# A fused graph-attention and transformer kernel: attention output normalised by VectorE 32x32 transposes, products begun with the high half, a new order, and no products of ones

## The chip, the cores and the metric

The kernel runs on one core of a Trainium2 chip (trn2). The metric is device microseconds of that core for one execution; the median of the runs of the kernel before is 545.64 us. Engines: TensorE (PE) multiplies, its weight loads have rows of their own (PEld), VectorE (DVE), ScalarE (ACT) and GpSimd (POOL) do element-wise work, SyncE (SP) issues the DMAs. SBUF is the on-chip memory, PSUM holds what TensorE writes, in 8 banks of 128 x 512 words.

## What is computed

Eight batches `b` of a sequence of S = 256 rows by D = 256 features go through two layers, all in fp32:

```python
# layer 0: graph attention over the first 20 rows, H = 16 heads of 16
self_feat = [x, q] @ W_self.T + b_self
for d in range(2):                      # adjacency and its transpose
    aff = softmax(mask(qh . kh / 4) + label_bias)      # 256 x 16 x 20
    output += (aff @ kv) @ Wout[d] + bout[d]
x = x + relu(self_feat + output)
# layer 1: transformer block
nx = rmsnorm(x) * weight * (1 + scale) + shift
q, k, v = rope(nx @ wq + bq), rope(nx @ wk + bk), nx @ wv + bv
attn = softmax(q . k / 4) @ v           # 16 heads, 256 x 256 each
x = x + attn @ wo + bo
nx = rmsnorm(x) * weight2 * (1 + scale2) + shift2
x = x + (gelu(nx @ w_gate) * (nx @ w_up)) @ w_down      # D_FF = 1024
```

## The kernel before, in words

Each fp32 operand of a large product is split into a high half (rounded to fp32r) and a low half (the rest). `product` (L1485) makes a product of three fp32r matmuls per 128-deep slice of the contraction: high x high, high x low, low x high. ACT or DVE makes the high half, POOL mostly the low one (`xl`, `selfl`, `nxl`, `nzl`, `hlow`, all by `low`, L409), and TensorE waits for the low half before a product's first matmul.

The order of every engine's work is written out by hand as a list of steps: `head`, then `round_(it)` for it = 2 to 6, then `tail`, joined by `program`. A round works on four batches at once: layer 0 of batch it+1 (`selfm`, `kv0`, `q0`, `affm`) and the end of layer 0 of batch it (`pTt`, `y`, `x1T`), queries, keys and values of batch it (`qk`, `qkT`) and it-1 (`v`), attention of batch it-1 (`s`, `st`, `pv`) with the last heads of it-2, and the output product and feed-forward of batch it-2 (`wo`, `nzTr`, `gate`, `up`, `down`). Engines meet only by semaphores: each step waits for counters and adds to one.

Attention of one batch: `s(h)` (L1698) makes scores whose row maximum DVE takes (`mx`, L1178); `nmT` turns the negated maxima; `st(h)` (L1722) makes the transposed scores with the maximum folded in, ACT takes `exph` (L687), and `pv(g)` (L1737) multiplies four heads at a time with v, to which ones are appended so that the row sums come out too. The operands of `s` and `st` are two tiles, `kst` and `qst`, which SP rebuilds for each batch through DRAM (`store_hi`, `store_lo`, then the nine DMAs of `stack`, L288 and L291): `stack(b)` waits until `st(15)` of batch b-1 has read the tiles, and `s(0)` of batch b waits for all nine.

After `pv(3)` the output is still head by head and not divided by its sums. Before the change the way to `wo` is: ACT copies PSUM to `oT32` (`oc`, L693), TensorE transposes it in eight 128x128 blocks (`oT`, L1747), DVE takes reciprocals and multiplies (`onorm`, L1198, L1200) into `attn`, TensorE transposes back (`aT`, four blocks, L1542 by the helper `transposes`), ACT adds the bias and writes the high half (`ah`, L702), DVE the low half (`al`, L1207), and `wo` starts. Then `x2add` (L1217), `square2` (L713), `rms2` on POOL, `xr2_scaled` (L1129), `nzTr` (L1542), `nzc` (L722), `nzh`, `nzl`, and the feed-forward. `s(0)` of the next batch writes the PSUM bank that `oT` used, so it waits for `at_ok`.

`adjm` (L1024 to L1027) is DVE work of layer 0 that stands between `al` and `x2add` in each round. `warm(i, bank, n)` (L1531) issues n products of a 128x128 tile of ones with itself, whose result nobody reads: 15 such steps stand in the head, 7 in the tail, none in the rounds.

```python
def wo(c):
    def step(b):
        if b + 1 < B:
            pe.wait_ge(qk_ok.sem, qk_ok.at(b + 1, 1))
        else:
            pe.wait_ge(gelu_ok.sem, gelu_ok.at(b - 1))
        pe.wait_ge(al_ok.sem, al_ok.at(b))
```

## Time and profile before

| what | us |
|---|---|
| runs of the kernel before | 545.64, 543.8, 551.11 |
| the profiled execution, its own time | 545.3 |
| its span, first to last instruction | 543.5 |
| PE busy, share of the span | 487.7, 90% |
| DVE busy | 343.3, 63% |
| ACT busy | 250.3, 46% |
| POOL busy | 186.7, 34% |
| mean granted TensorE clock | 0.969 of full speed |

A matmul's row gives its latency, and matmuls overlap, so that busy time on PE is less than the sum of the rows. The steps of `program` give the stages: the head lasts to 123.7 us, the five rounds to 403.7 us (56.0 us each), the tail to the end. The first `pv(3)` of a batch is a good mark: in the middle rounds it comes at 294.98 and 351.03 us, one round apart.

### The profile page before, as it was taken

How to read it: one execution, taken by the hardware profiler on the slowest of the kernel's cores; microseconds unless marked ns; L12 is line 12 of the kernel's file. 1: busy time of each engine (PE TensorE's matmuls, PEld its weight loads, DVE VectorE, ACT ScalarE, POOL GpSimd, SP SyncE). 2: the span in 40 equal slices, each digit the busy share in tenths (PEclk: the TensorE clock that was granted, in tenths of full speed). 3: DMA queues.
4: the chain of work that ended last, by engine and by line, in shares of the span. 5: the costliest groups of instructions: out<-in, count | busy, mean ns of one | idle time of the engine just before them, and what ended most of it. 6: DMA issues, size and time to landing. Idle time of an engine off the chain costs nothing. (4 is left out here: it accounts for less than half of the span.)

```text
span 543.5 us, 10140 instructions
## 1 busy us (share of the span) xinstructions
PE 487.7 (90%) x3893; PEld 424.9 (78%) x3893; DVE 343.3 (63%) x612; ACT 250.3 (46%) x489; POOL 186.7 (34%) x170
## 2 busy tenths in 40 slices
PE   7978877888999899998999899989997998899887
PEld 7877776665899679967996799769976986697786
DVE  4865788685867686668766875787565843460211
ACT  2371341264437642763366336734663455327331
POOL 2074334154235323542354234422442240211022
PEclk9967998899999999999999999999999999889999
DMA  8460390009102720254024502370027006400000
GB/s 264 168 220 21 127 216 2 1 22 226 23 3 74 173 42 2 75 150 65 2 76 129 85 1 75 104 112 1 23 92 123 1 4 153 62 1 3 21 1 22
DMA packets 33424, 40.26 MB, mean 74 GB/s; under 512 B 3168, under 2 KB 28256, under 8 KB 33120
## 3 DMA queue, kind: packets, MB, share of 16 engines
...
q14 instruction: 16, 0.13, 0.1%
...
## 5 line engine op out<-in xcount | busy, mean ns | idle before, releaser
L1491 PE MATMUL ps<-splz,wh 128*128 128x256 f32 x512 | 99.2, 289 | 0.9 <-POOL splz L409 0.8
L1178 DVE TENSOR_REDUCE nm<-ps 128x2 f32<-128x512 f32 x128 | 84.4, 686 | 24.0 <-PE ps L1698 23.8
L687 ACT ACTIVATE ya<-ps 128x512 f32<-128x512 f32 x128 | 71.8, 597 | 31.6 <-PE ps L1722 29.8
L1491 PEld LDWEIGHTS ps<-splz,wh 128*128 128x128 f32 x512 | 81.2, 195 | 3.4 <-issue 3.3
L409 POOL TENSOR_TENSOR hs<-g,hs 128x512 fp32r<-128x512 f32 x32 | 41.3, 1292 | 98.4 <-ACT hs L745 98.4
L1491 PE MATMUL ps<-splz,wl 128*128 128x256 f32 x256 | 73.3, 286 | 0.0
L1698 PE MATMUL ps<-kst,qst 96*128 96x256 f32 x256 | 54.6, 313 | 6.3 <-DVE nm L1178 2.7
L1491 PE MATMUL ps<-wh,hs 128*128 128x256 f32 x256 | 54.3, 284 | 0.5 <-POOL hs L409 0.5
L1722 PE MATMUL ps<-qst,kst 100*128 100x256 f32 x256 | 49.5, 303 | 2.7 <-ACT ya L687 2.1
L1491 PEld LDWEIGHTS ps<-splz,wl 128*128 128x128 f32 x256 | 49.8, 195 | 0.0
L1698 PEld LDWEIGHTS ps<-kst,qst 96*128 96x128 f32 x256 | 40.0, 199 | 12.3 <-DVE nm L1178 6.7
L1722 PEld LDWEIGHTS ps<-qst,kst 100*128 100x128 f32 x256 | 37.0, 189 | 15.1 <-ACT ya L687 9.7
L1491 PEld LDWEIGHTS ps<-wh,hs 128*128 128x128 f32 x256 | 43.2, 191 | 1.0 <-POOL hs L409 0.6
L1491 PE MATMUL ps<-splx,wh 128*128 128x256 f32 x192 | 38.6, 296 | 3.2 <-DVE wl L992 2.1
L1229 DVE TENSOR_TENSOR g<-ps,g 128x512 f32<-128x512 f32 x32 | 21.9, 685 | 27.3 <-PE ps L1491 27.3
L1737 PE MATMUL ps<-ya,vv 128*32 128x256 f32 x512 | 34.3, 385 | 4.3 <-ACT ya L687 4.3
L1491 PE MATMUL ps<-wh,sply 128*128 128x256 f32 (+1 forms) x128 | 37.5, 352 | 0.3 <-issue 0.3
L1536 PE MATMUL ps<-onesr 128*128 128x128 f32 x261 | 36.4, 293 | 1.0 <-POOL onesr L391 1.0
L1536 PEld LDWEIGHTS ps<-onesr 128*128 128x128 f32 x261 | 34.6, 210 | 3.0 <-issue 2.0
L735 ACT ACTIVATE g<-ps 128x512 f32<-128x512 f32 x32 | 19.0, 594 | 37.7 <-PE ps L1491 37.7
L1491 PE MATMUL ps<-wl,hs 128*128 128x256 f32 x128 | 36.2, 283 | 0.0
L437 POOL TENSOR_TENSOR prob<-aff,arc 128x640 f32<-128x640 f32 x16 | 22.2, 1388 | 40.5 <-DVE arc L1097 24.9
...
## 6 DMA issues: line engine op xcount, KB each, us to landing
...
```

The costliest lines, as they stand in the source:

```text
L409: pool.tensor_tensor(into, whole, high.bitcast(FP32), ALU.subtract).then_inc(signal.sem, 1)
L437: pool.tensor_tensor(prob[:, :, 0:M], aff[:, c].rearrange("p d h m -> p (d h) m"), arc[:, c, :].unsqueeze(2).broadcast_to([P, 2 * H, M]), ...
L687: act.activation(ex[:, h % EXR], ps[:, h % 2].rearrange("p (c s) -> p c s", c=TC), ACT.Exp, scale=SCALE).then_inc(ex_ok.sem, 1)
L735: act.activation(g32[:, j % 2], ps[:, BANK["g"]].rearrange("p (k s) -> p k s", k=2), ACT.Gelu).then_inc(gelu_ok.sem, 1)
L1178: dve.tensor_reduce(nm[:, :, h], ps[:, h % 2].rearrange("p (c s) -> p c s", c=TC), AX.X, ALU.max, negate=True).then_inc(mx_ok.sem, 1)
L1229: dve.tensor_tensor(g, ps[:, BANK["u"]].rearrange("p (k s) -> p k s", k=2), g, ALU.mult).then_inc(hm_ok.sem, 1)
L1491: ins = pe.matmul(dst, lhs(a, k), rhs(c, k), start=first_ and n == 0 and m == 0, stop=last_ and n == len(ks) - 1 and m == 2, **kw)
L1536: pe.matmul(ps[:, bank, 0:P], onesr[:], onesr[:], start=True, stop=True)
L1698: ins = pe.matmul(ps[:, h % 2, c * S:(c + 1) * S], qst[0:96, h // 2, c * P:(c + 1) * P], kst[0:96, h, :], start=True, stop=True)
L1722: ins = pe.matmul(ps[:, h % 2, c * S:(c + 1) * S], kst[0:100, h, c * P:(c + 1) * P], qst[0:100, h // 2, :], start=True, stop=True)
L1737: ins = pe.matmul(ps[32 * j:32 * j + 32, BANK["o"], (g % 2) * S:(g % 2 + 1) * S], vv[b % 2][:, c, h, :], ex[:, h % EXR, c, :], start=c == ...
```

## The change

- **Normalisation.** `oc`, `oT` and `aT` are gone. DVE reads the PSUM of `pv` by one `dve.transpose` of 32x32 blocks (`ot(n)`, 128x512, twice a batch), takes reciprocals and multiplies in SBUF, and transposes back (128x256, twice a batch). `ah` and `al` are split in two halves and read SBUF. The rows of `wo` and of the bias are permuted on the host to fit.
- **High half first.** `product` issues the matmuls that need only the fresh operand's high half, then waits for the low half (`low()`), then the rest. Every product has one more wait, in its middle.
- **Last batch.** `rest(b)` gives batch 7 other buffers and banks for `wo` and the feed-forward. There, DVE makes the high and low halves of `hs` and the low half of `n` that ACT and POOL made.
- **Order.** All five lists are rewritten; `s(0)` of the next batch no longer waits for the normalisation, `nmT` waits for `o_ok`.
- **Products of ones.** All of `warm` is gone.

```diff
+        rest_before = Rest(splz, splz, nz32, x2, xr2, 5, 6)
+        rest_last = Rest(splx, sply, self32[:], x1, xr, 3, 4)
...
-            def oc(n):
...
-                    act.activation(oT32[:, 2 * n:2 * n + 2, :], ps[:, 2].rearrange("p (g s) -> p g s", g=2), ACT.Copy).then_inc(o_ok.sem, 1)
...
-            def ah(b):
-                act.wait_ge(aT_ps.sem, aT_ps.at(b))
...
+            def ah(n):
+                def step(b):
+                    act.wait_ge(aT_ok.sem, aT_ok.at(b, n + 1))
+                    if b == B - 1:
+                        act.wait_ge(q0_ps.sem, q0_ps.at(b))
...
+                    act.activation(rest(b).o[:, 0, n, :], aT[:, n], ident_fn, bias=vec[:, V_BV + n:V_BV + n + 1]).then_inc(ah_ok.sem, 1)
...
-            def onorm(c):
-                def step(b):
-                    dve.wait_ge(oT_ps.sem, oT_ps.at(b, c + 1))
...
+            def ot(n):
+                def step(b):
+                    dve.wait_ge(pv_ps.sem, pv_ps.at(b, 2 * n + 2))
+                    dve.transpose(ob[:, n].rearrange("p g b v -> p (g b v)"), ps[:, BANK["o"]]).then_inc(o_ok.sem, 1)
+                return step
+
+            def onorm(n):
+                def step(b):
+                    dve.wait_ge(o_ok.sem, o_ok.at(b, n + 1))
+                    dve.reciprocal(orc[:, n], ob[:, n, :, :, DH]).then_inc(orc_ok.sem, 1)
+                    dve.wait_ge(orc_ok.sem, orc_ok.at(b, n + 1))
+                    dve.tensor_tensor(attn[:].rearrange("p b g d -> p g b d"), ob[:, n, :, :, 0:DH],
+                                      orc[:, n].unsqueeze(3).broadcast_to([P, 2, S // 32, DH]), ALU.mult).then_inc(at_ok.sem, 1)
+                    dve.wait_ge(at_ok.sem, at_ok.at(b, n + 1))
+                    dve.transpose(aT[:, n], attn[:].rearrange("p b g d -> p (b g d)")).then_inc(aT_ok.sem, 1)
+                return step
...
             def hmul(j):
...
+                    if b == B - 1:
+                        dve.wait_ge(hm_ok.sem, hm_ok.at(b, j + 1))
...
+                        high(hs[:, j % 2, 0], g, hh_ok)
+                        dve.wait_ge(hh_ok.sem, hh_ok.at(b, j + 1))
+                        dve.tensor_tensor(hs[:, j % 2, 1], g, hs[:, j % 2, 0].bitcast(FP32), ALU.subtract).then_inc(hl_ok.sem, 1)
...
-            def product(dst, lhs, rhs, ks, first_=True, last_=True, **kw):
-
-                for n, k in enumerate(ks):
-                    for m, (a, c) in enumerate(((0, 0), (0, 1), (1, 0))):
...
+            def product(dst, lhs, rhs, ks, halves, low, first_=True, last_=True, **kw):
+
+
+                high_, low_ = halves
+                todo = [(k, at) for k in ks for at in high_] + [(k, low_) for k in ks]
+                for n, (k, (a, c)) in enumerate(todo):
+                    if n == 2 * len(ks):
+                        low()
+                    ins = pe.matmul(dst, lhs(a, k), rhs(c, k), start=first_ and n == 0, stop=last_ and n == len(todo) - 1, **kw)
                 return ins
+
+
+            FED, HELD = (((0, 0), (1, 0)), (0, 1)), (((0, 0), (0, 1)), (1, 0))
...
-            def warm(i, bank, n):
...
-                    pe.wait_ge(nxl_ok.sem, nxl_ok.at(b))
+                    pe.wait_ge(nxh_ok.sem, nxh_ok.at(b))
...
-                            range(KC)).then_inc(qk_ps.sem, 1)
+                            range(KC), HELD, lambda: pe.wait_ge(nxl_ok.sem, nxl_ok.at(b))).then_inc(qk_ps.sem, 1)
...
-                        pe.wait_ge(at_ok.sem, at_ok.at(b - 1, h + 1))
+                        pe.wait_ge(ex_ok.sem, ex_ok.at(b - 1, H - 1 + h))
...
-                    pe.wait_ge(al_ok.sem, al_ok.at(b - 1))
+                    pe.wait_ge(o_ok.sem, o_ok.at(b - 1))
...
-            def oT(c):
...
-            def aT(b):
...
-                        pe.wait_ge(gelu_ok.sem, gelu_ok.at(b - 1))
-                    pe.wait_ge(al_ok.sem, al_ok.at(b))
+                        pe.wait_ge(x1_ok.sem, x1_ok.at(b))
+                    pe.wait_ge(ah_ok.sem, ah_ok.at(b))
```

**PE around `pv(3)` of batch 3, in the middle rounds.** Before (L1737 is `pv`, L1621 `pTt`, L1747 `oT`, L1542 on `ya` `aT`, L1491 any `product`, on `sply` it is `v(1)`, on `splz` `wo`):

```order
L1737 MATMUL ps<-ya,vv 32x256 x8
L1621 MATMUL ps<-const_sb,prob 128x128 x4
L1747 MATMUL ps<-const_sb,ya 128x128 x8
L1621 MATMUL ps<-const_sb,prob 128x128 x4
L1542 MATMUL ps<-const_sb,ya 128x128 x4
L1491 MATMUL ps<-wh,sply 128x256
```

Now (L1779 is `pv`, L1663 `pTt`, L1538 `product`):

```order
L1663 MATMUL ps<-const_sb,prob 128x128 x4
L1779 MATMUL ps<-ya,vv 32x256 x8
L1663 MATMUL ps<-const_sb,prob 128x128 x4
L1538 MATMUL ps<-wh,sply 128x256
L1538 MATMUL ps<-wl,sply 128x256
```

Twelve transposes have gone, one `pTt` has moved ahead of `pv(3)`, and between `pv(3)` and the output product only one `pTt` and `v(1)` are left.

**PE a little later, up to `s(0)` of batch 4.** Before (L1632 is `y`, L1554 `rsum`, L1542 on `l` `x1T`, on `xr` `nzTr`, L1698 `s`; the products on `sply` are `v(0)`):

```order
L1632 MATMUL ps<-l,vblk 64x256 x8
L1554 MATMUL ps<-splx,onesr 128x256 x4
L1542 MATMUL ps<-const_sb,l 128x128 x4
L1491 MATMUL ps<-wh,sply 128x256
L1491 MATMUL ps<-wl,sply 128x256
L1491 MATMUL ps<-wh,sply 128x256 x2
L1491 MATMUL ps<-wl,sply 128x256
L1491 MATMUL ps<-wh,sply 128x256
L1698 MATMUL ps<-kst,qst 128x256 x2
L1542 MATMUL ps<-const_sb,xr 128x128 x4
```

Now (L1674 `y`, L1582 `transposes`, L1596 `rsum`, L1740 `s`):

```order
L1674 MATMUL ps<-l,vblk 64x256 x8
L1582 MATMUL ps<-const_sb,l 128x128 x4
L1596 MATMUL ps<-splx,onesr 128x256 x4
L1582 MATMUL ps<-const_sb,xr 128x128 x4
L1740 MATMUL ps<-kst,qst 128x256 x2
```

`v(0)` has moved from ahead of `s(0)` to behind it, and `nzTr` from behind it to ahead.

**DVE in the same place, from `asums(1)` to `x2add`.** Before (L1095 and L1097 are `asums`, L1103 `pTv`, L1198 and L1200 `onorm`, L1207 `al`, L1024 the first of `adjm`):

```order
L1095 TENSOR_REDUCE asum<-aff 128x32
L1097 RECIPROCAL arc<-asum 128x32
L1103 COPY l<-ps 128x4x128
L1198 RECIPROCAL orc<-ps 128x16
L1200 TENSOR_TENSOR ya<-ps,orc 128x256
L1198 RECIPROCAL orc<-ps 128x16
L1200 TENSOR_TENSOR ya<-ps,orc 128x256
L1103 COPY l<-ps 128x4x128
L1207 SCALAR_TENSOR_TENSOR splz<-ps,vec,splz 128x256 x2
L1024 TENSOR_TENSOR aff<-adjD,wb 128x880
```

Now (L1208 is `ot`, L1214, L1216 and L1219 `onorm`, L1110 `pTv`, L1225 `al`):

```order
L1110 COPY l<-ps 128x4x128
L1208 STREAM_TRANSPOSE ya<-ps 128x512
L1214 RECIPROCAL orc<-ya 128x16
L1216 TENSOR_TENSOR attn<-ya,orc 128x2x8x16
L1219 STREAM_TRANSPOSE ya<-attn 128x256
L1225 SCALAR_TENSOR_TENSOR splz<-ya,vec,splz 128x256
L1110 COPY l<-ps 128x4x128
L1225 SCALAR_TENSOR_TENSOR splz<-ya,vec,splz 128x256
L1031 TENSOR_TENSOR aff<-adjD,wb 128x880
```

`ot(0)` and `onorm(0)` stand earlier, on either side of `klow` and `result`; `ot(1)` and its `onorm` stand behind `asums(1)` and `pTv(0)`, and `adjm` is still ahead of `x2add`.

**PE at the end, batch 7.** Before, seven steps of ones stand around the chain:

```order
L1536 MATMUL ps<-onesr 128x128 x6
L1737 MATMUL ps<-ya,vv 32x256 x8
L1747 MATMUL ps<-const_sb,ya 128x128 x8
L1536 MATMUL ps<-onesr 128x128 x6
L1542 MATMUL ps<-const_sb,ya 128x128 x4
L1536 MATMUL ps<-onesr 128x128 x12
L1491 MATMUL ps<-wh,splz 128x256
```

Now `pv(3)` is followed by `wo` at once, which reads `splx`:

```order
L1764 MATMUL ps<-qst,kst 128x256 x4
L1779 MATMUL ps<-ya,vv 32x256 x8
L1538 MATMUL ps<-wh,splx 128x256
L1538 MATMUL ps<-wl,splx 128x256
L1538 MATMUL ps<-wh,splx 128x256
```

The two fillers behind `wo` (24 and 20 products) and the one ahead of the last two `down` (5) have gone as well.

## Rows read from the trace of the kernel before

**Rows 1.** The page, part 2: 40 slices of 13.6 us, granted clock in tenths.
```profile
PEclk9967998899999999999999999999999999889999
```

**Rows 2.** Windows: start:end, length, busy us (x instructions) by engine, PEclk, DMA.
```profile
291.74:347.79 56.05, 52.93 (x449) 46.19 (x448) 40.24 (x72) 29.42 (x59) 21.41 (x20) 1.00 0.29 71
...
294.99:307.89 12.90, 10.38 (x89) 7.97 (x89) 8.98 (x18) 3.99 (x10) 3.43 (x4) 1.00 0.84 163
307.89:351.03 43.14, 42.55 (x361) 38.22 (x359) 31.25 (x56) 25.44 (x49) 17.98 (x15) 1.00 0.13 43
```

**Rows 3.** Groups by shape: out<-in xcount | busy us, mean ns | idle before, releaser.
```profile
L1747 PE MATMUL ps<-const_sb,ya 128*128 128x128 f32 x64 | 8.5, 276 | 2.1 <-ACT ya L693 2.1
L1198 DVE RECIPROCAL orc<-ps 128x16 f32<-128x16 f32 x16 | 4.0, 251 | 18.9 <-PE ps L1747 18.9
L1200 DVE TENSOR_TENSOR ya<-ps,orc 128x256 f32<-128x256 f32 x16 | 6.8, 424 | 0.6
L702 ACT ACTIVATE splz<-ps,vec 128x256 fp32r<-128x256 f32 x16 | 6.7, 471 | 20.3 <-PE ps L1542 20.3
L1103 DVE COPY l<-ps 128x512 f32<-128x512 f32 x16 | 10.8, 672 | 6.2 <-PE ps L1621 6.0
L1536 PE MATMUL ps<-onesr 128*128 128x128 f32 x261 | 36.4, 293 | 1.0 <-POOL onesr L391 1.0
```

**Rows 4.** Timeline around the lull of batch 3: start, us, engine, line.
```profile
299.49 0.92 SPq L291 DMA_DIRECT2D kst<-qk_d  x2
301.34 1.06 DVE L1024 TENSOR_TENSOR aff<-adjD,wb 128x880 f32<-128x880 int32 x1
304.28 0.68 DVE L1217 TENSOR_TENSOR x<-ps,x1b 128x512 f32<-128x512 f32 x1
307.89 0.40 PE L1698 MATMUL ps<-kst,qst 96*128 96x256 f32 x2
308.23 0.63 PE L1542 MATMUL ps<-const_sb,xr 128*128 128x128 f32 x4
```

**Rows 5.** Timeline, the rebuilding of `kst` for batch 7.
```profile
459.88 0.93 SPq L291 DMA_DIRECT2D kst<-qk_d  x2
468.77 0.71 PE L1698 MATMUL ps<-kst,qst 96*128 96x256 f32 x4 [0.65 <-DMA kst<-qk_d]
```

**Rows 6.** Windows, columns as in rows 2: stretches around changes of the clock.
```profile
89.70:93.10 3.40, 1.27 (x11) 1.24 (x11) 3.26 (x7) 0.00 (x0) 0.00 (x0) 1.00 0.00 0
304.80:308.20 3.40, 2.33 (x20) 1.93 (x17) 2.20 (x7) 1.71 (x6) 2.16 (x3) 1.00 0.38 55
468.60:472.00 3.40, 2.73 (x14) 1.84 (x14) 3.25 (x7) 1.51 (x3) 0.38 (x2) 1.00 0.00 0
472.00:478.90 6.90, 6.55 (x29) 6.29 (x30) 2.84 (x5) 1.88 (x2) 1.00 (x1) 0.51 0.00 0
```

**Rows 7.** Timeline of the end, batch 7.
```profile
506.89 0.60 ACT L693 ACTIVATE ya<-ps 128x512 f32<-128x512 f32 x1 [1.19 <-PE ps L1737]
512.34 0.36 PE L1491 MATMUL ps<-wh,splz 128*128 128x256 f32 x1 [0.64 <-DVE splz L1207]
519.76 1.26 POOL L409 TENSOR_TENSOR splz<-g,splz 128x512 fp32r<-128x512 f32 x1 [3.02 <-DVE splz L955]
521.17 0.47 PE L1491 MATMUL ps<-splz,wh 128*128 128x256 f32 x2 [0.82 <-POOL splz L409]
537.08 0.67 PE L1536 MATMUL ps<-onesr 128*128 128x128 f32 x5
538.20 0.39 PE L1491 MATMUL ps<-wh,hs 128*128 128x256 f32 x1 [0.46 <-POOL hs L409]
```

**Rows 8.** Timeline of the head, queries and keys of batch 0.
```profile
56.75 1.27 POOL L409 TENSOR_TENSOR sply<-xr,sply 128x512 fp32r<-128x512 f32 x1 [2.96 <-DVE sply L955]
58.12 0.47 PE L1491 MATMUL ps<-wh,sply 128*128 128x512 f32 x1 [0.27 <-issue]
60.98 0.40 PE L1491 MATMUL ps<-splx,wh 128*128 128x256 f32 x2
```

More of the change, by code:

```diff
@@ L1 @@
+import collections
 import math
@@ L300, in store @@
                 sp.wait_ge(res_ok.sem, res_ok.at(b))
-                sp.dma_start(out[b].rearrange("(c p) d -> p c d", p=P), res[:]).then_inc(res_out.sem, 16)
+                sp.dma_start(out[b].rearrange("(c p) d -> p c d", p=P), rest(b).xr2[:]).then_inc(res_out.sem, 16)
             get_consts = fetch(consts[:], consts_in, consts_arr)
@@ L712, in square2 @@
                 for c in range(TC):
-                    act.activation(xr2[:, c], x2[:, c], ACT.Square, accum_out=ss2[:, c:c + 1]).then_inc(ss2_ok.sem, 1)
+                    act.activation(rest(b).xr2[:, c], rest(b).x2[:, c], ACT.Square, accum_out=ss2[:, c:c + 1]).then_inc(ss2_ok.sem, 1)
             def nzc(b):
@@ L1204, in al @@
-            def al(b):
-                dve.wait_ge(ah_ok.sem, ah_ok.at(b))
-                for k in range(KC):
-                    ins = dve.scalar_tensor_tensor(out=spla[:, 1, k, :], in0=ps[:, BANK["aT"], k * S:(k + 1) * S], scalar=vec[:, V_BV + k:V_BV + k + 1],
-                                                   in1=spla[:, 0, k, :].bitcast(FP32), op0=ALU.add, op1=ALU.subtract)
-                ins.then_inc(al_ok.sem, 1)
+                    dve.wait_ge(pv_ps.sem, pv_ps.at(b, 2 * n + 2))
+                    dve.transpose(ob[:, n].rearrange("p g b v -> p (g b v)"), ps[:, BANK["o"]]).then_inc(o_ok.sem, 1)
@@ L1211, in x2add, with al @@
+            def al(n):
+                def step(b):
+                    dve.wait_ge(ah_ok.sem, ah_ok.at(b, n + 1))
+                    dve.scalar_tensor_tensor(out=rest(b).o[:, 1, n, :], in0=aT[:, n], scalar=vec[:, V_BV + n:V_BV + n + 1],
+                                             in1=rest(b).o[:, 0, n, :].bitcast(FP32), op0=ALU.add, op1=ALU.subtract).then_inc(al_ok.sem, 1)
+                return step
             def x2add(b):
@@ L1216, in x2add @@
                     dve.wait_ge(w_low[part].sem, w_low[part].at(0, n + 1))
[L1217 removed]
+                dve.tensor_tensor(rest(b).x2[:], ps[:, rest(b).wo_bank].rearrange("p (c d) -> p c d", c=TC), x1b[:], ALU.add).then_inc(x2_ok.sem, 1)
             def nzh(b):
@@ L1221, in nzh @@
                 dve.wait_ge(wo_ps.sem, wo_ps.at(b))
-                high(splz[:, 0], nz32, nzh_ok)
+                if b == B - 1:
+                    dve.wait_ge(qk_ps.sem, qk_ps.at(b))
+                    dve.wait_ge(v_ps.sem, v_ps.at(b))
+                high(rest(b).n[:, 0], rest(b).n32, nzh_ok)
+                if b == B - 1:
+                    dve.wait_ge(nzh_ok.sem, nzh_ok.at(b))
+                    dve.tensor_tensor(rest(b).n[:, 1], rest(b).n32, rest(b).n[:, 0].bitcast(FP32), ALU.subtract).then_inc(nzl_ok.sem, 1)
             def hmul(j):
@@ L1528, in cond_2 @@
                 return step
-            def warm(i, bank, n):
-                def step():
-                    if i == 0:
-                        pe.wait_ge(onesr_ok.sem, onesr_ok.at(0))
-                    for _ in range(n):
-                        pe.matmul(ps[:, bank, 0:P], onesr[:], onesr[:], start=True, stop=True)
-                return step
             def transposes(dst, src, signal):
@@ L1983, in round_ @@
-                q0(1, 1)(it + 1)
-                up(3, 1)(it - 2)
-                q0(1, 0)(it + 1)
-                up(3, 0)(it - 2)
-                nxT(it)
-                affm(0)(it + 1)
-                st(0)(it - 1)
-                down(1, 0)(it - 2)
-                down(1, 1)(it - 2)
+                up(2, 0)(it - 2)
+                q0(0, 0)(it + 1)
+                s(15)(it - 1)
+                gate(3, 0)(it - 2)
+                gate(3, 1)(it - 2)
+                q0(1, 1)(it + 1)
@@ L1992, in round_ @@
+                q0(1, 0)(it + 1)
+                nmT(it - 1)
+                up(2, 1)(it - 2)
+                down(0, 0)(it - 2)
+                down(0, 1)(it - 2)
+                affm(0)(it + 1)
+                nxT(it)
+                up(3, 0)(it - 2)
+                down(1, 0)(it - 2)
+                st(0)(it - 1)
+                up(3, 1)(it - 2)
                 st(1)(it - 1)
@@ L2040, in tail @@
                 s(4)(6)
+                gate(0, 0)(5)
                 s(5)(6)
@@ L2043, in tail @@
                 s(6)(6)
-                gate(0, 0)(5)
                 s(7)(6)
@@ L2137, in tail @@
                 up(2, 0)(6)
+                gate(3, 1)(6)
+                nmT(7)
                 up(2, 1)(6)
-                nmT(7)
                 down(0, 0)(6)
+                down(0, 1)(6)
                 gate(3, 0)(6)
-                gate(3, 1)(6)
-                down(0, 1)(6)
                 up(3, 0)(6)
```

604 lines of the change are left out of this document (284 added, 320 removed).

## The prediction

> **What bounds the kernel now.** I read the page first, then windows by stage, then the timeline of one round, and last the timelines of the end and the head. The page's clock line shows TensorE at full speed from the fourth slice of the head on but for a few slices [rows 1]. A middle round takes 56.05 us, and PE is busy for 52.93 of them, DVE for 40.24, ACT for 29.42, POOL for 21.41 [rows 2]. So PE is the bound, but not evenly. From `s(0)` of batch 4 to the next `pv(3)` it is busy for 42.55 of 43.14 us: there only less PE work or a faster clock helps. From `pv(3)` of batch 3 to that `s(0)` it is busy for 10.38 of 12.90 us [rows 2]; I call this the lull. In it a chain sets the time: `pv(3)`, normalisation, `wo`, `adjm`, `x2add`, norm, `nzTr`. The reader is to see that all that the change takes from PE in a round, the twelve transposes, stands in the lull, where PE is not the limit, so that what counts there is when `s(0)` can come and not how much PE does.
>
> **Own time.** The profiled execution took 545.3 us, 1.8 more than its span of 543.5, and 0.3 less than the median of 545.64. The sum is made on 545.3.
>
> **The transposes in a round.** `oT` is eight transposes for each of eight batches, 8.5 us in all with 2.1 us of waiting [rows 3], so 1.3 us a batch; `aT` has half as many, 0.5 us at the same price. The way by DVE costs two transposes of 128x512 from PSUM, two reciprocals, two multiplications and two transposes of 128x256. The trace has no DVE transpose. The nearest row is the PSUM copy of 128x512 at 0.672 us [rows 3]; for 128x256 I take the multiplication's 0.424. From below I bound them by half of the copy, 0.34, from above by a GpSimd pass over 128x512, 1.27 us [rows 8]. I take the copy's price, being the same shape from the same bank.
> The page "Vector Engine (DVE) Microarchitecture Reference" of the Trainium skill, section 3.8, says that the 32x32 transpose passes one element per cycle and lane; no run here shows it yet, and by it the price would be about the copy's.
>
> The lull of one batch, counted from the start of `pv(3)`, which I take to come at the same point, since the exponentials ahead of it are the same: PSUM is complete after 1.2 us (at the end ACT, whose last exponential `pv(3)` needs, idles for 1.19 us until it can copy the result [rows 7]). `ot(1)` has `asums(1)` and `pTv(0)` ahead of it on DVE and starts at about 1.4; 0.67 for it, 0.25, 0.42 and 0.42 for the rest [rows 3] and some gaps bring 3.3; `ah(1)` at 0.47 [rows 3] brings 3.9, and the first `wo` starts. The low half (`al(1)`, behind `al(0)` and `pTv(1)`) is there at 4.8, after the four matmuls with the high half, a wait of 0.4. Behind `al(1)` DVE runs `adjm`, from 301.34 to 304.28 before [rows 4], 2.9 us, so `x2add` starts at 7.8. Before, it started at 304.28 - 294.99 = 9.3 [rows 2, 4]. From `x2add` to `nzTr` it was 308.23 - 304.28 = 3.95 us [rows 4] and stays that, since squares, `x1bias` and the norm are unchanged: `nzTr` at 11.75, and `s(0)`, now right behind, at 12.2 instead of 12.9. That is 0.7 us earlier. But `v(0)`, six matmuls at 0.12 (twelve of twice the columns take 60.98 - 58.12 = 2.86 us [rows 8]), 0.72 us, has moved from the lull into the dense part, and `nzTr`, four transposes, about 0.4, out of it. So the dense part grows by 0.3 and a batch gains about 0.4 us, not the 1.8 us of PE work removed. Six batches (0 to 5) have such a lull: -2.4 us.
> How much more could it be? `s(0)` needs `kst`, rebuilt after `st(15)`. At the end of the rounds it visibly waits for that: last pair issued at 459.88, `s(0)` at 468.77 with an idle time of 0.65 us put to the DMA, 8.9 us later [rows 5]. In the middle round the last pair goes out at 299.49 [rows 4]; 8.9 us more is 308.4, past the 307.89 at which `s(0)` started without such a wait, so this landing was quicker, but the room is small. `store` and `load_x_add`, which change places around `stack` in SP's list, are one DMA each and don't move it. I allow at most 1.0 us a batch, -6 in all, and at worst +1.1 a batch, +6.6, if the transposes take twice the copy.
>
> **The lull's clock.** This is the term against the change. The clock was at its upper level (2.4 GHz) in 89.70 to 93.10, with PE busy for 1.27 of 3.40 us, and at the lower one (1.2 GHz) right behind [rows 6]; it also fell after 468.60 to 472.00, where PE was busy for 2.73 of 3.40 us, for 6.9 us in which 29 matmul records took 6.55 us of PE. But it held through 304.80 to 308.20 at 2.33 of 3.40 [rows 6]. So the lulls were near the edge already, and now lose twelve transposes each. A fall costs half of the time spent at the lower level where PE is dense, 3.4 us of 6.9. I expect half of one such fall over the six lulls: +1.7 us. Bounds: 0, and six times 1.7 = +10.
> The page "TensorE: Matmul & The Clock Gate" of the Trainium skill says, in "What's actually happening", that the clock falls after an idle stretch. By that rule alone no lull would cost anything, since PE is never idle throughout one, and the sum would be 1.7 us less; the fall behind 468.60 to 472.00, at 2.73 busy of 3.40, speaks against it, and I keep the row's side.
>
> **High half first.** It adds one wait to each of 36 products a batch, in the middle of matmuls at 0.12 us. `s` and `gate` already have one or two waits each and, where those are satisfied, run at the same 0.12, so I take nothing; from above 0.02 us each would be 0.7 a batch and +5 in all. What it gives stands where a product waited for a low half: in the head `qk(0)` starts at 58.12, just after `nxl` (56.75 + 1.27) [rows 8], so up to -1.3. In the dense part PE waits for no low half, and it gives nothing.
>
> **Batch 6.** Its lull ends on the `kst` landing [rows 5], which no edit moves: 0. The filler behind `wo` goes; the clock fell there even with it.
>
> **The end.** After `pv(3)` of batch 7, PSUM complete at 506.89 [rows 7]: 0.67, 0.25, 0.42, 0.42, `ah` 0.47 and gaps of 0.2 put `wo` at 509.4, not 512.34: -2.9. `gate` no longer waits for POOL: it may start when that subtraction started, 519.76, instead of 521.17, -1.4, and then waits some 0.2 for DVE's low half, which is shorter. At the very end the last two `down` started 538.20 - 537.08 = 1.1 us after the ones ahead of them were issued [rows 7]; with the halves on DVE at about 0.45 and 0.7 they are in time: -1.1. Together -5.2. Against it: between `pv(3)` and the first `gate` PE now has twelve matmuls and four transposes in 10 us, less than the stretch that kept the clock up [rows 6]. So `wo` and the first gates run at the lower level. By the 6.9 us of the fall [rows 6] that is 3.4 us; with some of `wo`, +3.5. Bounds: 0 to +8.5, if it stays low for the whole feed-forward of 17 us. The end gives -1.7.
>
> **The head.** Fillers go from gaps, so their 36.4 us [rows 3] are no gain: they stood where PE waited. What they did was to hold the clock, which was at the upper level from 48.8 to 82.9. `qk(0)` and `qk(1)` of batch 0, from 58.12 to 60.98 [rows 8], stand on the chain to `s(0)`; at the lower level they take 2.9 us more. The four `q0` ahead of the first softmax (0.72 each) would add 2.9 too; since PE is dense there and the clock would recover on the way, half: 1.5. Less the 1.3 of the high half: +3.1. Bounds -3 (the clock holds, and the new DMA order helps) to +10 (everything PE does to 103 us is slower). Where DVE's row maxima pace the first `s`, the clock costs nothing.
>
> Sum: -2.4 + 1.7 + 0 - 1.7 + 3.1 = +0.7, 546.0 us.
>
> **The rivals.** First, *the chain pays more than I think*: DVE transposes are cheap, the lulls shrink by the full 1.0 us (-6), the clock holds in lulls and head (head -3), and the end keeps its -5.2. That is -14.2, 531.1 us. For it: idle time on DVE in the round (16 of 56 us), and an end in which all is chain. Against: the `kst` landing and the fillers, which stood where the clock was seen to fall. Chance 0.17.
> Second, *the clock decides, and the kernel is slower*. Place: the lulls, where the transposes no longer fill. Price: 1.7 us for a fall with one half of 3.4 us dense behind it. From the point at which the lulls fall in four of six batches (+6.8, and less the 1.7 counted) and the head pays the +8 of its clock, it is 546.0 + 5.1 + 4.9 = 556.0, and with all six and the end's 8.5 some 564. Chance 0.15 for more than 2% slower.
> Third, *the change to DVE does not relieve the bound at all*: the DVE chain behind `pv(3)` is late by `asums` and `pTv`, `s(0)` comes as before, and the round grows by `v(0)`: +0.3 a batch instead of -0.4, 550 us. It lies within my own case's range.
>
> **How the numbers follow.** My case, within 2% (534.7 to 556.6; about what a measurement of this kernel can tell from no change), 0.68; the first rival 0.17 beyond that on the fast side; the second 0.15 on the slow side. The forecast is 546 us. My case's bounds alone are 538 to 555. For 8 in 10 the range goes half way into both rivals: 533 to 560.
>
> **What would show it.** Right: rounds of 55 to 56 us; `s(0)` about 12.2 us behind `pv(3)`; DVE transposes of 128x512 near 0.67 us; the clock lower than 0.969 in the mean, with falls in the head and behind `pv(3)` of batch 7; the last `gate` stage starting 3 to 4 us nearer to `pv(3)`. Wrong: rounds under 54.5 us, which would mean that the dense part has shrunk, and I have nothing that shrinks it; or lulls at the lower clock in most rounds; or a row for a DVE transpose over 1 us; or products with a gap in the middle in the dense part.

## The result and the profile after

The changed kernel takes 548.76 us (median of 20 runs, 544.53 to 552.56), the kernel before beside it 545.26 us (20 runs, 542.88 to 552.18): a ratio of 1.006, 95% interval 1.0039 to 1.0081. It is slightly slower. The forecast was 546.0, "within 2%". The profiled execution took 548.7 us, with a span of 546.9.

The page of after, first the engines, then the clock line, the counterpart of [rows 1]:

```profile
PE 460.4 (84%) x3536; PEld 399.8 (73%) x3536; DVE 381.2 (70%) x653; ACT 240.3 (44%) x469; POOL 185.6 (34%) x165
...
PEclk9955957589999989999999989998999999999869
```

PE does 27 us less, DVE 38 us more. The clock line has more low digits in the head and near the end, and single 8s in the rounds, where the line of before had none.

Windows of after: the lull of batch 1 and the dense part behind it, which ran at full clock, the same pair of batch 3, whose dense part began at the lower clock, then four stretches at the lower clock: the one behind the lull of batch 4, two in the head, one at the end (start:end, length, busy us by engine, PEclk, DMA; a PEclk of 1.00 is 2.4 GHz, 0.50 is 1.2 GHz). They answer to [rows 2] and [rows 6].

```profile
189.04:201.66 12.62, 9.21 (x71) 7.25 (x71) 10.85 (x19) 2.84 (x8) 4.69 (x5) 0.86 0.69 138
201.66:245.74 44.08, 43.28 (x368) 38.95 (x367) 34.78 (x59) 25.71 (x49) 17.67 (x14) 1.00 0.16 52
303.98:316.95 12.97, 8.56 (x71) 6.52 (x71) 10.92 (x19) 2.85 (x8) 4.68 (x5) 0.97 0.78 126
316.95:362.19 45.24, 44.45 (x367) 40.11 (x365) 34.59 (x58) 25.71 (x49) 17.67 (x14) 0.97 0.16 51
...
374.20:377.60 3.40, 3.18 (x15) 3.21 (x16) 2.06 (x5) 1.22 (x3) 0.50 (x1) 0.50 0.00 0
29.50:56.80 27.30, 19.91 (x91) 17.15 (x90) 16.52 (x27) 11.09 (x22) 14.93 (x12) 0.50 0.37 127
70.40:87.50 17.10, 10.18 (x43) 9.51 (x44) 11.79 (x17) 5.25 (x10) 11.61 (x9) 0.50 0.88 158
514.20:527.80 13.60, 7.25 (x31) 6.65 (x32) 3.72 (x8) 4.05 (x9) 0.88 (x2) 0.50 0.00 0
```

The reader is to see three things. The lull is 12.6 to 13.0 us, against 12.90 before, although PE's work in it went from 10.38 to about 9: PE's work does not set its length, a chain does. The dense part grew from 43.14 to 44.08 us, and to 45.24 where its start ran at the lower clock (granted clock 0.97 in the mean; the fifth line shows such a stretch by itself, 3.40 us at 0.50, behind the lull of batch 4). And head and end have long stretches at 0.50.

The groups of after that took the place of `oT`, `aT` and the old `onorm` of [rows 3]:

```profile
L1216 DVE TENSOR_TENSOR attn<-ya,orc 128x256 f32<-128x256 f32 x16 | 13.4, 840 | 0.5
L1208 DVE STREAM_TRANSPOSE ya<-ps 128x512 f32<-128x512 f32 x16 | 11.4, 710 | 16.7 <-PE ps L1779 16.7
L1219 DVE STREAM_TRANSPOSE ya<-attn 128x256 f32<-128x256 f32 x16 | 7.1, 445 | 0.5
```

The transposes cost what was forecast (0.71 and 0.45 us for 0.67 and 0.42). The multiplication costs 0.84 us where the same shape cost 0.424 before. The timelines of POOL and of DVE in the lull of batch 3, the counterpart of [rows 4], show why:

```profile
305.99 1.30 POOL L418 TENSOR_TENSOR splx<-xT,splx 128x512 fp32r<-128x512 f32 x1
```
```profile
305.88 0.25 DVE L1214 RECIPROCAL orc<-ya 128x16 f32<-128x16 f32 x1
306.16 1.40 DVE L1216 TENSOR_TENSOR attn<-ya,orc 128x256 f32<-128x256 f32 x1
307.60 0.45 DVE L1219 STREAM_TRANSPOSE ya<-attn 128x256 f32<-128x256 f32 x1
```

The multiplication starts at 306.16, while GpSimd's `xl` runs until 307.29, and ends 0.27 us behind it. It is 1.40 us in batches 0 to 4; in batches 5 to 7, which have no `xl` beside it, it is 0.42. The first multiplication of a batch meets GpSimd too, for less long. In batch 3 (POOL, then DVE):

```profile
299.94 1.72 POOL L432 TENSOR_TENSOR aff<-aff,amx 128x640 f32<-128x640 f32 x1
```
```profile
301.33 0.62 DVE L1216 TENSOR_TENSOR attn<-ya,orc 128x256 f32<-128x256 f32 x1
```

It too ends 0.3 us behind the GpSimd operation. The multiplication of before, with one operand in PSUM, ran its first 0.24 us beside a GpSimd operation as well, and took no longer than its mean of 0.424:

```profile
296.79 1.27 POOL L437 TENSOR_TENSOR prob<-aff,arc 128x640 f32<-128x640 f32 x1 [3.13 <-PE ps L1621]
```
```profile
297.82 0.42 DVE L1200 TENSOR_TENSOR ya<-ps,orc 128x256 f32<-128x256 f32 x1
```

The end, for [rows 7] (PE, then DVE's first transpose behind `pv(3)`):

```profile
511.60 1.07 PE L1779 MATMUL ps<-ya,vv 128*32 128x256 f32 x16 [0.94 <-ACT ya L696]
515.37 0.55 PE L1538 MATMUL ps<-wh,splx 128*128 128x256 f32 x1 [2.70 <-ACT splx L707]
...
521.78 1.09 PE L1582 MATMUL ps<-const_sb,xr 128*128 128x128 f32 x4 [3.52 <-DVE xr L1141]
524.54 0.55 PE L1538 MATMUL ps<-sply,wh 128*128 128x256 f32 x1 [1.66 <-DVE sply L962]
```
```profile
512.74 0.72 DVE L1208 STREAM_TRANSPOSE ya<-ps 128x512 f32<-128x512 f32 x1 [2.65 <-PE ps L1779]
```

`wo` starts 3.77 us behind `pv(3)`, before 6.59; `gate` 12.94 us behind it, before 15.42.

For every trace I read the same marks off PE's timeline, the starts of `pv(3)`, `s(0)` and the last `down(3,1)` (us; "end" is `pv(3)` of b7 to the last `down(3,1)`, "lull" is `pv(3)` to `s(0)`, "dense" is `s(0)` to `pv(3)`):

| kernel | median | pv(3) of b0 | b0 to b5 | b5 to b7 | end | lull b3 | dense b2 |
|---|---|---|---|---|---|---|---|
| before | 545.26 | 126.78 | 280.27 | 98.70 | 33.27 | 12.91 | 43.15 |
| after | 548.76 | 132.34 | 288.00 | 91.25 | 30.83 | 12.97 | 44.08 |
| fill_lulls | 543.69 | 130.74 | 283.57 | 92.09 | 30.98 | 12.63 | 44.09 |
| fill_ends | 539.64 | 126.69 | 286.48 | 91.36 | 28.31 | 12.97 | 44.04 |
| before_bare | 550.88 | 130.45 | 280.64 | 99.07 | 36.31 | 12.90 | 43.17 |
| xl_early | 540.95 | 132.75 | 278.61 | 92.35 | 31.39 | 11.65 | 44.08 |
| dense_back | 546.69 | 130.50 | 285.66 | 92.68 | 30.94 | 12.98 | 44.01 |
| low_old | 557.85 | 133.22 | 293.23 | 94.28 | 32.31 | 14.74 | 44.88 |
| last_plain | 550.86 | 131.37 | 287.39 | 91.60 | 31.73 | 12.62 | 44.09 |
| combo1 | 537.44 | 127.18 | 281.81 | 92.13 | 28.42 | 12.38 | 43.97 |
| best2 | 535.51 | 130.02 | 278.64 | 92.91 | 28.39 | 11.64 | 44.09 |
| best3 | 540.66 | 127.23 | 285.86 | 92.25 | 28.33 | 12.25 | 45.11 |
| best4 | 539.37 | 128.39 | 281.76 | 92.86 | 28.41 | 12.17 | 44.52 |
| best5 | 528.72 | 128.37 | 275.08 | 93.24 | 28.43 | 10.66 | 44.10 |

From before to after the four stretches change by +5.56, +7.74, -7.45 and -2.44, in sum +3.4 us. The question for the experiments is what these four are.

### The profile page after: what moved, and what is told of

It is laid out like the page before. It is cut to its first block and busy times, and to the rows that moved or that the text cites. A ratio compares the mean times of both kernels' runs of the same rounds, so it can differ in the third digit from the quotient of the medians.

```text
span 546.9 us, 9419 instructions
## 1 busy us (share of the span) xinstructions
PE 460.4 (84%) x3536; PEld 399.8 (73%) x3536; DVE 381.2 (70%) x653; ACT 240.3 (44%) x469; POOL 185.6 (34%) x165
## 5 line engine op out<-in xcount | busy, mean ns | idle before, releaser
L1538 PE MATMUL ps<-splz,wh 128*128 128x256 f32 x448 | 97.4, 286 | 0.0
L1538 PEld LDWEIGHTS ps<-splz,wh 128*128 128x128 f32 x448 | 76.0, 190 | 0.3 <-ACT g L744 0.2
L1740 PE MATMUL ps<-kst,qst 96*128 96x256 f32 x256 | 56.9, 324 | 5.3 <-DMA kst<-qk_d 2.5
L1538 PE MATMUL ps<-splz,wl 128*128 128x256 f32 x224 | 58.3, 282 | 0.0
L1764 PE MATMUL ps<-qst,kst 100*128 100x256 f32 x256 | 52.7, 307 | 3.0 <-issue 1.7
L1538 PE MATMUL ps<-wh,hs 128*128 128x256 f32 x256 | 54.5, 283 | 0.0
L1740 PEld LDWEIGHTS ps<-kst,qst 96*128 96x128 f32 x256 | 42.3, 210 | 13.8 <-DVE nm L1189 7.4
L1538 PE MATMUL ps<-splx,wh 128*128 128x256 f32 x192 | 47.9, 321 | 5.1 <-DVE wl L999 3.9
L1538 PEld LDWEIGHTS ps<-wh,hs 128*128 128x128 f32 x256 | 43.3, 190 | 0.2
L1538 PEld LDWEIGHTS ps<-splx,wh 128*128 128x128 f32 x192 | 38.7, 228 | 6.4 <-issue 6.3
L1538 PEld LDWEIGHTS ps<-splz,wl 128*128 128x128 f32 x224 | 42.7, 191 | 0.0
L1538 PE MATMUL ps<-wh,sply 128*128 128x256 f32 (+1 forms) x128 | 41.0, 370 | 0.8 <-ACT xr L664 0.6
L1779 PE MATMUL ps<-ya,vv 128*32 128x256 f32 x512 | 34.3, 385 | 6.0 <-ACT ya L696 6.0
L1663 PE MATMUL ps<-const_sb,prob 128*128 128x128 f32 x128 | 22.8, 316 | 14.9 <-POOL prob L446 14.9
L1538 PE MATMUL ps<-wl,hs 128*128 128x256 f32 x128 | 33.4, 282 | 0.0
L432 POOL TENSOR_TENSOR aff<-aff,amx 128x640 f32<-128x640 f32 x16 | 23.5, 1467 | 23.1 <-DVE amx L1096 23.1
```

The source lines that it names most:

```text
L432: pool.tensor_tensor(t, t, amx[:, c, :].unsqueeze(2).broadcast_to([P, 2 * H, M]), ALU.subtract).then_inc(asub_ok.sem, 1)
L1538: ins = pe.matmul(dst, lhs(a, k), rhs(c, k), start=first_ and n == 0, stop=last_ and n == len(todo) - 1, **kw)
L1663: ins = pe.transpose(ps[:, BANK["pT"][d], g * P:(g + 1) * P], prob[:, at:at + 4, :].rearrange("p h m -> p (h m)"), ident)
L1740: ins = pe.matmul(ps[:, h % 2, c * S:(c + 1) * S], qst[0:96, h // 2, c * P:(c + 1) * P], kst[0:96, h, :], start=True, stop=True)
L1764: ins = pe.matmul(ps[:, h % 2, c * S:(c + 1) * S], kst[0:100, h, c * P:(c + 1) * P], qst[0:100, h // 2, :], start=True, stop=True)
L1779: ins = pe.matmul(ps[32 * j:32 * j + 32, BANK["o"], (g % 2) * S:(g % 2 + 1) * S], vv[b % 2][:, c, h, :], ex[:, h % EXR, c, :], start=c == ...
```

## The experiments

Fillers are products of ones, written as the old `warm`; all edits are to the changed kernel unless said otherwise.

**fill_lulls.**

```diff
                 pv(3)(it - 2)
+                warm(31, 0, 8)()
...
                 v(1)(it - 1)
+                warm(32, 0, 8)()
...
                 y(it)
+                warm(33, 0, 8)()
...
                 rsum(it + 1)
+                warm(34, 0, 8)()
```

> The changed kernel with products of ones put back, but only in the rounds, at four gaps of each lull (eight each: behind pv(3), v(1), y and rsum), 160 in all. Theory A, the clock costs the rounds 1.2 to 1.4 us for each of the four falls that follow a lull: the falls at 193, 258, 316 and 374 us go, s(0) to the next pv(3) takes 44.1 us in all rounds instead of 45.2 to 45.4, and the time is about 5 us below the changed kernel's 548.8, near 544. Theory B, the dense part has grown by moved work alone and the falls are harmless: the falls go and the time stays at 548 to 549. Theory C, the fillers run into the chain behind pv(3): the lulls grow by 0.3 us or more, and the time is 550 or more.

543.69 us, 0.9949 of before (0.9919 to 0.9979). Windows, to be held against the lull and the dense part at 303.98 and 316.95 of after:

```profile
300.85:313.48 12.63, 11.95 (x101) 9.89 (x102) 10.85 (x19) 2.88 (x8) 4.70 (x5) 1.00 0.72 130
313.48:357.56 44.08, 43.31 (x368) 38.99 (x366) 34.73 (x59) 25.71 (x49) 17.69 (x14) 1.00 0.15 52
```

Theory A. PE does 11.95 us in a lull that is no longer for it, and the clock holds through all rounds. Batch 0 to 5 takes 4.43 us less, three falls of 1.5 us. There were four in after; the one at 193.30 lies wholly in its lull, where PE waits anyway, and cost nothing (12.62 us, against 12.63 here).

**fill_ends.** Fillers in the head and the tail alone, at the gaps of the new order, for instance:

```diff
                 pv(3)(7)
+                warm(17, 0, 22)()
                 wo(0)(7)
                 wo(1)(7)
+                warm(19, 0, 26)()
```

> The changed kernel with products of ones put back in the head (about where they stood before, 175 of them) and in the last two lulls and the end (113), none in the rounds. Theory A, the clock: pv(3) of batch 0 comes at 127 to 128 us again instead of 132.3, the end gains 1.5 to 2 us, and the time is near 548.8 - 4.5 - 1.7 = 542.6. Theory B, the head is late by its new order of DMAs and steps and not by its clock: pv(3) of batch 0 stays at 131 to 132, and the time is 547 or more.

539.64 us, 0.9887 (0.9843 to 0.9931). Theory A, and more than expected: `pv(3)` of batch 0 is back at 126.69, so all of the head's 5.56 us went with the fillers; the end takes 28.31 us instead of 30.83. Two falls are left in the rounds, so that batch 0 to 5 takes 1.5 us less. The stretch from `pv(3)` to `gate`, which had a granted clock of 0.60 in after, now reads:

```profile
504.53:515.73 11.20, 10.28 (x95) 9.36 (x95) 4.55 (x11) 2.78 (x8) 0.88 (x2) 1.00 0.01 1
```

**before_bare.** The kernel before without any `warm`, for instance:

```diff
                 nzTr(7)
-                warm(20, 4, 20)()
                 gate(0, 0)(7)
```

> The kernel before with all its products of ones taken out and nothing else. Theory A: the head loses 4.5 us and the end 2 us, 545.3 + 6.5 = 552. Theory B, the fillers were worth nothing: 545.3. If this is as slow as 552, then what the changed kernel gains elsewhere is about 3 us.

550.88 us, 1.0093 (1.0059 to 1.0126), +4.6 us beside its own runs of before. The trace has +3.67 in the head and +3.04 in the end. Theory A, with the head less dear than in the changed kernel.

**xl_early.**

```diff
                 asub(1)(it)
+                xl(it + 1)
                 aprob(1)(it)
-                xl(it + 1)
                 x1bias(it - 1)
```

> The changed kernel with one line of GpSimd's list moved: the low half of x (xl of the next batch) goes out ahead of aprob(1) and not behind it, so that it no longer runs at the same time as VectorE's second multiplication of the normalisation. Theory A, the multiplication waits for the GpSimd subtraction that runs beside it: it takes 0.42 us again in batches 0 to 4 instead of 1.40, wo comes 1 us sooner, each lull ends up to 1 us sooner, and the time is up to 5 us lower, 544 to 546 (less where s(0) then meets the landing of kst). Theory B, the multiplication is slow by its own access pattern: it stays at 1.40 us and the time at 548 to 549.

540.95 us, 0.9901 (0.9863 to 0.9940): 7.8 us off after's 548.8 for one moved line. The group of the multiplication, and POOL and DVE in the lull of batch 3:

```profile
L1216 DVE TENSOR_TENSOR attn<-ya,orc 128x256 f32<-128x256 f32 x16 | 8.6, 535 | 0.5
```
```profile
297.60 1.47 POOL L418 TENSOR_TENSOR splx<-xT,splx 128x512 fp32r<-128x512 f32 x1
```
```profile
302.13 0.43 DVE L1216 TENSOR_TENSOR attn<-ya,orc 128x256 f32<-128x256 f32 x1
```

Theory A: 0.43 us with nothing beside it, and each lull exactly 0.97 us shorter (11.65). Against fill_lulls, which has no falls either, batch 0 to 5 takes 4.96 us less, five times 0.99. The rest of the gain is that no fall came in the rounds any more; I had not expected that, and why the clock held was not tested. PE does 8.19 us in such a lull of 11.65, and did 8.56 in one of 12.97.

**dense_back.**

```diff
-                pTt(1)(it)
                 pv(3)(it - 2)
+                pTt(1)(it)
...
                 rsum(it + 1)
+                v(0)(it - 1)
                 nzTr(it - 2)
...
-                v(0)(it - 1)
                 s(1)(it - 1)
```

The tail has the same two moves, for batch 5.

> The changed kernel with two of TensorE's steps put back from the dense part of a round into the lull, where they stood before: pTt(1) behind pv(3), and v(0) between rsum and nzTr (also in batch 5's lull). Theory A, the dense part grew by exactly these, 0.54 + 0.72 us, less the 0.38 of nzTr: s(0) to the next pv(3) falls from 44.1 to 42.8 us, the lull stays at 12.6, and as TensorE is busier in the lulls the falls behind them go too: 6 x 1.26 + 3 x 1.5 = 12 us, 537. Theory B, the lull is full already (v(0) ends late and holds s(0)): the lull grows by 0.7 us and the time is 544 to 549.

546.69 us, 1.0009 (0.9974 to 1.0045). Neither: the dense part stays, the falls in the rounds go, and the lull grows by half of what theory B says. The windows, and PE's waits in the dense part and at the `pv(3)` that ends it:

```profile
187.53:200.50 12.97, 9.47 (x80) 7.29 (x81) 11.21 (x19) 3.01 (x8) 4.86 (x5) 1.00 0.70 130
200.50:244.51 44.01, 42.45 (x359) 37.94 (x357) 34.70 (x59) 25.70 (x48) 17.68 (x14) 1.00 0.17 53
```
```profile
PE ps L1779 <- ACT ya L696: 1.1, 1, 1.1
PE ps L1538 <- POOL splz L418: 0.3, 1, 0.3
```

After has only the first of the two waits, and so had before:

```profile
PE ps L1779 <- ACT ya L696: 0.7, 1, 0.7
```
```profile
PE ps L1737 <- ACT ya L687: 0.5, 1, 0.5
```

PE does 0.83 us less in the dense part and the dense part stays at 44.0. In after, `pTt(1)` filled a part of the wait of `pv(3)` for the last exponential, and `v(0)` the wait of `gate(0,0)` for its low half. Take them out and the waits are 0.7 us longer. So the dense part was not bound by PE alone, though its busy share was 98%. The last `st` starts 42.5 us behind `s(0)` in after and 42.4 in dense_back, against 41.8 before: the way to the last exponential is longer by the same amount with the two steps and without them, and what in the new order lengthens it no run shows. In the lull `v(0)` then held up `nzTr` by 0.35 us.

**low_old.**

```diff
-                todo = [(k, at) for k in ks for at in high_] + [(k, low_) for k in ks]
+                todo = [(k, at) for k in ks for at in (*high_, low_)]
                 for n, (k, (a, c)) in enumerate(todo):
-                    if n == 2 * len(ks):
+                    if n == 0:
                         low()
```

> The changed kernel with product undone: the wait for the low half stands ahead of a product's first matmul again, and the matmuls go slice by slice; 36 waits in the middle of products are gone. Theory A (the prediction's): the waits cost nothing where they are satisfied, what high half first gives is 1.3 us at qk(0) of the head and 0.4 us in each lull and at the end: 548.8 + 1.3 + 2.8 = 553. Theory B: each wait in the middle costs 0.02 us, 5 us in all, and the time is 545 to 547 after what is lost in the lulls. Theory C: nothing either way, 548 to 549.

557.85 us, 1.0221 (1.0175 to 1.0267), 9.1 us over after, more than any theory had. PE's longest wait in the lull of batch 1 (in after it is the 1.2 us for the high half, ACT L707), and the two windows:

```profile
PE ps L1538 <- DVE splz L1225: 2.0, 1, 2.0
```
```profile
191.91:205.45 13.54, 9.31 (x71) 7.39 (x71) 10.94 (x19) 2.79 (x8) 4.69 (x5) 0.87 0.66 121
205.45:250.32 44.87, 43.75 (x371) 39.07 (x371) 34.84 (x59) 25.79 (x49) 17.68 (x14) 1.00 0.15 52
```

High half first is worth 0.9 us in this lull and 0.8 in this dense part. What the waits in the middle of products cost can't be read from this run, since it takes their gain away with them; the gain is larger in every stretch. The 9.1 us are not the waits for low halves alone. From `pv(3)` of batch 0 to that of batch 5 the clock is at the lower level for 23.9 us, in after for 13.7, so a part is the clock's. And in the dense part PE's wait for a low half is only 0.2 us, while PE is busy 0.5 us longer; the edit also changes the order of a product's matmuls, and no run parts the two.

**last_plain.** The last batch with the common buffers, banks and engines (`rest` gives `rest_before` for every batch), its steps on POOL and ACT in the order of before.

```diff
-            return rest_last if b == B - 1 else rest_before
+            return rest_last if b == -1 else rest_before
```

> The changed kernel with the last batch like the others: its output product and feed-forward use the common buffers and banks, ACT makes hs's high half and GpSimd the low halves of n and hs. Theory A (the prediction's terms for gate, -1.4 + 0.2, and for the last down, -1.1): the way from pv(3) of batch 7 to the last down is 2.3 us longer, 33.1 instead of 30.8, and the time 551. Theory B: the subtraction on VectorE takes as long and the last halves are hidden: no more than 0.5 us, 549.

550.86 us, 1.0080 (1.0041 to 1.0118), not to be told from after by its time. In the trace `gate` comes 12.9 us behind `pv(3)` in both, and the end is 31.73 instead of 30.83. So the last batch's own buffers and engines give 0.9 us, behind `gate`, and nothing at `gate`: between the theories.

**combo1.** The edits of fill_ends, xl_early and dense_back together.

> Three edits together: the products of ones in head and end (fill_ends), xl ahead of aprob(1) (xl_early), and pTt(1) and v(0) back in the lull (dense_back). If they add up: 539.6 from the first; then 1.0 a lull for five batches and the two falls of 1.5 us that the first still had, -8; then 1.26 for six batches, -7.6: 524. If the landing of kst binds s(0) or v(0) holds it in the shorter lull, 1 us a round less comes out, 529 or more.

537.44 us, 0.9856 (0.9814 to 0.9897). Not 524: dense_back gives nothing here either, and costs 0.74 us a lull (12.38 against 11.65).

**best2.** fill_ends and xl_early alone.

> xl ahead of aprob(1) (xl_early) and the products of ones in head and end (fill_ends), without the two steps put back in the lull. Theory A, the gains add since they lie in different stretches: xl_early's 7.8 us and fill_ends' 9.2 us off 548.8, or 539.6 less five lulls of 0.97 and two falls of 1.5, 531.8. Each lull is 11.65 us, 0.75 less than in combo1, where v(0) held nzTr. Theory B: the shorter lull meets the landing of kst, and no more than combo1's 537.4 is reached.

535.51 us, 0.9787 (0.9733 to 0.9841). Lulls of 11.64 us, no fall in the rounds, the end at 28.39: the gains add in those stretches. `pv(3)` of batch 0 came at 130.02, not 126.69, with fillers in the same places: the clock was at the lower level from 91.8 to 105.5 us, in fill_ends only from 98.8 to 102.2. That is 3.3 of the 3.7 us by which the sum is missed; what let the clock fall there in one and not in the other no run shows.

**best3.** best2 with one more edit in GpSimd's list (and the same for the two batches of the tail):

```diff
                 aprob(1)(it)
-                x1bias(it - 1)
                 rms2(it - 2)
+                x1bias(it - 1)
```

> best2, and in GpSimd's list rms2 of a batch ahead of x1bias of the next one. x1bias took 1.27 us from 313.09 to 314.36 while the squares for rms2 were there at 313.88. Theory A: the inverse root comes 0.5 us sooner and with it xr2_scaled, nzTr and s(0); 0.5 us for seven lulls, 3.5 us below best2, 528. Theory B, s(0) is bound by something else by now (x1T behind yadd, or kst's landing): 0 to 1 us.

540.66 us, 0.9888 (0.9845 to 0.9932): 5 us slower than best2, which no theory had. `xr2_scaled` in the lull of batch 3, in best2 (with no GpSimd work beside it) and then in best3 with its neighbour on POOL:

```profile
307.69 0.62 DVE L1141 TENSOR_SCALAR xr<-x,r 128x256 f32<-128x256 f32 x2 [1.46 <-POOL r L455]
```
```profile
308.98 1.26 POOL L470 TENSOR_TENSOR x1b<-x,bo 128x512 f32<-128x512 f32 x1
```
```profile
309.04 1.61 DVE L1141 TENSOR_SCALAR xr<-x,r 128x256 f32<-128x256 f32 x2 [0.98 <-POOL r L455]
```

The inverse root is ready 0.5 us sooner behind `pv(3)`, but now `x1bias` runs beside `xr2_scaled` and makes it 1 us longer: a collision like that with `xl`, moved to another instruction. The lull grows to 12.25, and three falls of the clock came back (dense 45.1 to 45.5).

**best4.** best3 and, in TensorE's list:

```diff
                 pv(3)(it - 2)
+                v(0)(it - 1)
...
-                v(0)(it - 1)
...
-                gate(0, 0)(it - 2)
                 s(3)(it - 1)
+                gate(0, 0)(it - 2)
```

> best3, and in TensorE's list of the rounds v(0) right behind pv(3), in the gap of 1.2 us before pTt(2), and s(3) ahead of gate(0,0) so that work stands where gate waits for its low half. dense_back had shown that taking v(0) out of the dense part alone brings only 0.1 us of its 0.72, since gate(0,0) then waits 0.6 longer. Theory A: the dense part shrinks by v(0)'s 0.7 us with the lull unchanged, five rounds, 3.5 us below best3. Theory B: the row maxima on VectorE and the norm set the pace behind s(0), s(3) waits in gate's place, and 0 to 1 us is gained.

539.37 us, 0.9892 (0.9851 to 0.9933). Theory B: the dense part without a fall is 44.0 us against 44.08.

**best5.** best2 with `adjm` split:

```diff
                 x2add(it - 2)
+                adjw(it + 1)
                 yadd(it)
```

where `adjw` is `adjm`'s last reduction.

> best2, and the third of adjm's three operations on VectorE (1.06 us) moved from ahead of x2add to behind it, into the idle time before yadd. In best2, wo is done by 303.4 us and x2add starts at 304.50, behind adjm. Theory A, VectorE's list ahead of x2add sets the lull: x2add, the norm, nzTr and s(0) come 1.0 us sooner in five rounds, lulls of 10.65 us instead of 11.64, and the time is 5 us below best2's 535.5, 530.5, if no new falls of the clock follow. Theory B, s(0) then waits for kst, whose last DMA is issued at 299.47 and would have 8 us to land, as 8.9 were seen in the kernel before: 0.3 to 0.7 us of it is left, 532 to 534. Theory C: with x1bias beside it on GpSimd the moved reduction or yadd takes longer and nothing is gained, 535.5.

528.72 us, 0.9675 (0.9634 to 0.9717): 3.3% faster than the kernel before and the best of all. The lull of batch 3 and the dense part behind it:

```profile
293.90:304.56 10.66, 8.20 (x70) 6.16 (x71) 9.87 (x19) 2.85 (x8) 3.43 (x4) 1.00 0.93 152
304.56:348.67 44.11, 43.31 (x369) 38.99 (x367) 34.73 (x59) 25.71 (x49) 19.12 (x15) 1.00 0.15 52
```

Theory A in the lulls of batches 2 to 4: 0.98 us each, for a reduction that nobody needed there, and `kst`'s landing did not bind at 10.66 us. In the lull of batch 0 it did, as theory B has it: `nzTr` was through early, and `s(0)` waited for the DMA.

```profile
140.00 0.48 PE L1755 MATMUL ps<-kst,qst 96*128 96x256 f32 x2 [0.73 <-DMA kst<-qk_d]
```

That lull stayed at 11.63 us, and the one of batch 1 came to 10.93. Batch 0 to 5 takes 3.56 us less than in best2, not 4.9; the head was 1.65 us shorter too, which this edit does not explain.

## Why the prediction came out right, and where it was wrong

The number was right to 0.5% and the class held, but by luck: several steps were wrong and cancelled. Of the signs named for being right, the rounds of 55 to 56 us did not come; from `pv(3)` of batch 0 to that of batch 5 they took 56.7 to 58.2.

- **The head**, +3.1: measured +5.56, within the bounds. The mechanism was right (fill_ends gives all of it back) and the size off. The prediction let the lower clock cost only `qk` and `q0`, and held that row maxima pace the first `s`; from `s(0)` of batch 0 to `nmT`, the delay grew from 1.6 to 4.1 us. And the -1.3 of the high half did not show as a net gain.
- **The lull**, -0.7 before `v(0)` and `nzTr`: measured -0.28 (12.62 for 12.90). The step that failed is the price of the multiplication, "0.42". It came from a row in which one operand lay in PSUM; now both lie in SBUF, and it waits for GpSimd. Without that (xl_early) the lull is -1.25. The first rival's full 1.0 us a batch did not come even so: it counted the dense part in, which took 0.9 back, and a round of xl_early is 55.72 us against 56.05, 0.33 less.
  The page "SBUF — State Buffer" of the Trainium skill, section "SBUF: two separate sides", says that a DVE instruction with two SBUF inputs, or in a mode that uses both ports, and a GpSimd instruction that reads SBUF hold a shared pair of ports as an exclusive lock. The traces agree: 1.40 us beside `xl` and 0.43 without it, 1.61 beside `x1bias` and 0.62 without it. Whether the multiplications by a scalar ran in such a mode no run shows. Read before the prediction the section would have named the first of these costs.
- **The dense part**, +0.3: measured +0.93 (44.08 for 43.15). The step left out `pTt(1)`, which also moved ahead of `pv(3)`, and with its 0.5 us the count of PE's work comes near to +0.9. But that is not the cause. The step's ground, that only PE's work counts there, fell with dense_back: both steps out, and still 44.0. The row of before had a sign of it, `pv(3)` waiting 0.5 us for an exponential at the end of the part. What else in the new order costs the 0.9 us stays open.
- **The lull's clock**, +1.7 for half a fall: there were four falls, of which three cost 1.5 us each, +4.4 in all. The price of a fall (1.7) was right, the number was not. "Lulls at the lower clock in most rounds" was named as a sign that the forecast is wrong, and it came: a fall in or behind four of the six lulls. That the time was still near is owed to the next point.
- **Batches 5 and 6**, -0.4 and 0: measured -7.45 from `pv(3)` of batch 5 to that of batch 7. In batch 5 neither `xl` nor `adjm` stands in the way, and its lull falls from 12.39 to 10.10 us. Of the rest, low_old has each of the two dense parts and batch 6's lull 0.8 us longer, which would be the high half's; and behind batch 6's lull the lower clock lasted 3.4 us instead of 6.9, about 1.7 us. These shares are a reading: no run took the new order apart in these two batches. "Which no edit moves: 0" for that lull was wrong: it went from 11.53 to 10.41. About 1 us stays with the new order, unassigned.
- **High half first**, nothing in the dense part: low_old is 9.1 us slower in all, falls of the clock included, and 0.8 in each dense part that has no fall in either. The prediction read the old kernel's waits, where no low half was late; in the new order `gate` and `wo` stand right behind their high halves, and there the edit pays. This is the largest error of reading, hidden because the order and the edit came together. (Its upper bound for the waits is also mis-summed: 0.7 us a batch is 5.8 in eight, not 5.)
- **The end**, -5.2 + 3.5 = -1.7: measured -2.44. With the clock held (fill_ends) it is -4.96, so the chain was right to 0.3 us (`wo` -2.8 for -2.9; `wo` to `gate` 7.43 for 8.83, -1.4 as said; the rest -0.7 for -1.1), and the clock cost 2.5 for 3.5. The gain at `gate` is not owed to the last batch's buffers and engines (last_plain), which fits the prediction's reason, that `gate` starts on its high half.

The second rival had the right mechanism, falls in four of six batches, but a head at +8 that did not come. Counted together, what fillers give back is 5.6 us in the head, 4.4 in the rounds (where no fillers had stood, but the twelve transposes) and 2.5 at the end, 12.6 us. The rest of the change gains some 9 us, and the collision with `xl` keeps back another 5.
